# Softmax sums from ScalarE's natural exponentials, folded into the shift, with attention scheduled query chunk by query chunk

## The reference

```python
xn = layernorm(x)
Q, K, V = xn @ Wq.T, xn @ Wk.T, xn @ Wv.T            # 16 heads of 32
S = einsum('bhqd,bhkd->bhqk', rope(Q), rope(K)) * 32 ** -0.5
S = where(causal, S, -inf)
heads = einsum('bhqk,bhkd->bqhd', softmax(S), V)
x = x + heads @ Wo.T + (silu(xn @ Wg.T) * (xn @ Wu.T)) @ Wd.T
```

## Time and profile before

| | us |
|---|---|
| median of 3 runs | 2245.01 (2243.44 to 2249.74) |
| the profiled execution, its own time | 2243.66 |
| its span | 2241.8 |
| PE, busy | 2034.9 (91%) |
| DVE, busy | 1176.1 (52%) |
| ACT, busy | 737.9 (33%) |
| POOL, busy | 760.3 (34%) |
| granted TensorE clock, mean | 0.978 |

### The profile page before, as it was taken

The page is one execution under the profiler, slowest core; times in us unless marked ns, Lnnn a source line. Parts: engine busy times, 40 slices in busy tenths (PEclk is TensorE's granted clock), DMA queues, the critical chain, the costliest instruction groups (busy, mean ns, idle before and its releaser), DMA issues.

```text
span 2241.8 us, 34912 instructions
## 1 busy us (share of the span) xinstructions
PE 2034.9 (91%) x10176; PEld 1352.9 (60%) x10176; DVE 1176.1 (52%) x2458; ACT 737.9 (33%) x1357; POOL 760.3 (34%) x552
## 2 busy tenths in 40 slices
PE   4999999999899999999869999999997999999996
PEld 3756657566475646476557576674755746464764
DVE  5635637355555646374357265472736537282733
ACT  2242332423323342423322423324242242415242
POOL 3324324242321515153323143431423215142523
PEclk9999999999899999999979999999998999999998
DMA  3313103041130303041123041220411303030403
GB/s 136 79 32 95 43 28 94 15 114 43 38 74 28 89 19 98 10 118 30 53 103 96 11 104 33 54 83 9 113 34 43 85 11 98 10 98 17 126 24 122
DMA packets 72428, 140.67 MB, mean 63 GB/s; under 512 B 9328, under 2 KB 26736, under 8 KB 71152
## 3 DMA queue, kind: packets, MB, share of 16 engines
q1 hardware_dynamic: 72304, 139.25, 22.2%
HBM read 75.77 MB, written 4.19 MB: 36 GB/s over the span
## 4 chain that ended last, share of the span: by engine, by line
PE 44%; issue 26%; POOL 15%; DVE 6%; ACT 2%; SPq 2%; DMA 2%; DVEq 1%; POOLq 1%; ACTq 1%
PE D L900 10%; PE G L900 8%; PE S L969 7%; PE O L986 6%; PE U L900 6%; PE E L993 3%; POOL pr L745 3%; POOL swapped L727 3%; POOL pr L733 2%; ACT pr L639 2%; POOL wgl L698 2%; POOL hl L721 2%; SPq L576 2%; POOL wul L698 1%; PE S L953 1%
## 5 line engine op out<-in xcount | busy, mean ns | idle before, releaser
L639 ACT ACTIVATE pr<-S 128x512 f32<-128x512 f32 (+3 forms) x768 | 341.1, 489 | 293.7 <-PE S L969 292.0
L868 DVE TENSOR_TENSOR xres<-D,xres 128x512 f32<-128x512 f32 x352 | 242.2, 688 | 347.4 <-PE D L900 341.3
L721 POOL TENSOR_TENSOR hl<-tt,hh 128x512 fp32r<-128x512 f32 x108 | 138.9, 1286 | 550.2 <-ACT hh L663 550.0
L969 PE MATMUL S<-QS,KS 98*128 98x512 f32 (+2 forms) x768 | 240.5, 388 | 11.4 <-DMA QS<-mt 5.7
L969 PEld LDWEIGHTS S<-QS,KS 98*128 98x128 f32 x768 | 132.8, 188 | 192.1 <-ACT pr L639 171.0
L663 ACT CAST hh<-tt 128x512 fp32r<-128x512 f32 x108 | 67.0, 620 | 481.8 <-DVE tt L882 481.8
L745 POOL TENSOR_SCALAR_AFFINE_SELECT pr<-pr 128x512 f32<-128x512 f32 x128 | 81.2, 635 | 379.7 <-ACT pr L639 379.7
L986 PE MATMUL O<-pr,vh 128*32 128x512 f32 (+3 forms) x1536 | 163.8, 498 | 46.4 <-POOL pr L745 45.5
L858 DVE RECIPROCAL denom<-denom 128x256 f32<-128x256 f32 x64 | 109.1, 1730 | 181.0 <-ACT denom L646 181.0
L900 PE MATMUL G<-xh,wgh 128*128 128x512 f32 x432 | 177.6, 411 | 14.2 <-DVE tt L879 10.6
L900 PE MATMUL D<-wdh,hh 128*128 128x512 f32 x432 | 180.1, 417 | 4.1 <-DVE xres L868 3.2
(11 more groups left out here) (137 smaller groups left out, 3737.6 us busy)
## 6 DMA issues: line engine op xcount, KB each, us to landing
KS<-pr SPq DMA_DIRECT2D x192, 128.0 KB, 2.3
QS<-pr SPq DMA_DIRECT2D x192, 128.0 KB, 2.3
raw<-in_wgate_dram SPq DMA_DIRECT2D x29, 512.0 KB, 3.5
raw<-in_wup_dram SPq DMA_DIRECT2D x28, 512.0 KB, 3.7
raw<-in_wdown_dram SPq DMA_DIRECT2D x28, 512.0 KB, 3.4
raw<-in_wqk_dram SPq DMA_DIRECT2D x18, 512.0 KB, 3.4
vh<-val SPq DMA_DIRECT2D x16, 512.0 KB, 3.8
val<-in_x_dram SPq DMA_DIRECT2D x6, 1024.0 KB, 10.3
```

Source lines behind the costliest of these rows:

```text
L639: act.activation(pr[:, (i * HG + h) % 8, skip:W], S[h % 2][:, skip:W], ACT.Exp, scale=SCALE) \
L721: pool.tensor_tensor(hl[:, fc, :], tt[:, (blk * nfc + fc) % 2, :], hh[:, fc, :].bitcast(F32), ALU.subtract) \
L868: dve.tensor_tensor(xres[:, rt, :], d[:, :], xres[:, rt, :], ALU.add).then_inc(sem["v_dfree"], 1)
L969: pe.matmul(S[h % 2][:, first:W], KS[0:SHIFT, h, kb * P:(kb + 1) * P], QS[0:SHIFT, h, c * W + first:(c + 1) * W], start=True, stop=True).t ...
```

## The change

Five things change together.

1. *Sums.* After VectorE's row extreme (now a minimum, since the factor -32^-0.5 is multiplied into Q in `proj` and `rotate`), ScalarE takes the exponential of each natural score block in place in PSUM, with the minimum as bias and the row sum as accumulator output. For the second chunk the two parts' sums are joined by a few small operations (`parts`, `joined`). Then `log`: ScalarE takes the logarithm and VectorE subtracts the minimum and splits the result into halves; `flip` transposes it with PE. There is one `log` and one `flip` for each chunk. The transposed scores are then shifted by maximum plus logarithm, so their exponentials are the softmax itself.
2. *Gone:* `sums` on PE, the copy of the denominators, the reciprocals, the multiplication of the heads. `heads` is now one cast on ScalarE (`ah`) and one subtraction on VectorE (`al`); GpSimd's part in it is gone.
3. *Buffers.* `pr` holds four sets (`RING`); the transposed scores take turns in three banks (S0, S1, E). `swapped` and `xn` lie in `pr`.
4. *Order.* Natural scores go chunk by chunk (16 products for queries 0 to 511, then 32), and values two sets at a time, behind the four scores of the next set. MLP pieces are spread by `paced` over natural and transposed scores in proportion to needs that `NEED_NAT` and `NEED_ST` state. The last two sets' values stand behind the first projection (`V` in `ENDS`).
5. *Weights.* The raw buffers are fixed by kind: A, O and U share buffer 0, G and D buffer 1. The split of A moves ahead of the natural scores, that of O to natural product 24.

The core of the diff:

```diff
+RING = 4
-    return [[("nat", h, u)] for h in range(HG) for u in range(len(NAT))]
+    items = [([("nat", t)], NEED_NAT[w_ // P - 1]) for t, (_, _, _, _, w_) in enumerate(NAT)]
+    n0 = sum(x[0] == 0 for x in NAT)
+    items[n0 + 3][0].append(("log", 0))
+    items[n0 + 7][0].append(("flip", 0))
...
+NEED_NAT = (3, 4, 4, 4)
+NEED_ST = (2, 2, 3, 3)
+EDGE = {"turn0": (8, 4), "turn1": (6, 4), "tail0": (10, 14), "tail1": (7, 10)}
+ENDS = ("pVpwwxpxxpwwxpD", "pVpwwxpxxpwwxpD")
-SLOTS = {"open0": "", "turn0": "A0 G1 U0 O1 D0 G1 U0 D1", "tail0": "A0 G1 U0 O1 D0 G1 U0 D1",
-         "open1": "", "turn1": "O1 A0 G0 U1 D0", "tail1": "O1 A0 G1 U0 D1 G0 U1 D0 G1 U0 D1"}
+SLOT = {"A": 0, "O": 0, "U": 0, "G": 1, "D": 1}
...
 @block.scalar
+            def nat(n, t):
+                c, h, qb, part, w_ = NAT[t]
+                act.wait_ge(sem["v_max"], n("v_max", 1))
+                s, at = NB[t % 4][:, 0:w_], h * TPC + qb % TPC
+                act.activation(s, s, ACT.Exp, bias=mp[:, c + part, at:at + 1], scale=-1.0,
+                               accum_out=se[:, c + part, at:at + 1]).then_inc(sem["a_nat"], 1)
+            def log_(n, c):
+                if c:
+                    act.wait_ge(sem["v_join"], n("v_join"))
+                else:
+                    act.wait_ge(sem["a_nat"], n("a_nat"))
+                act.activation(lse[:, :], se[:, 0, :], ACT.Ln).then_inc(sem["a_log"], 1)
...
-                act.wait_ge(sem["p_pv"], n("p_pv"))
+                act.wait_ge(sem["p_pv"], n.at("p_pv", i - RING + 1))
-                act.copy(heads[:, :], O[:, :])
-                act.copy(denom[:, :], E[:, :]).then_inc(sem["a_heads"], 1)
+                act.wait_ge(sem["p_wo"], n("p_wo"))
+                act.copy(ah[:, :], O[:, :]).then_inc(sem["a_ah"], 1)
...
 @block.vector
+            def log_(n, c):
+                dve.wait_ge(sem["a_log"], n("a_log", 1))
+                dve.wait_ge(sem["p_flip"], n("p_flip"))
+                dve.tensor_tensor(lse[:, :], lse[:, :], low_[:, :] if c else mp[:, 0, :], ALU.subtract).then_inc(sem["v_lse"], 1)
...
+                dve.tensor_copy(mm[:, 0, :].bitcast(F32R), lse[:, :]).then_inc(sem["v_lse"], 1)
...
+                dve.tensor_tensor(mm[:, 1, :], lse[:, :], mm[:, 0, :], ALU.subtract).then_inc(sem["v_lse"], 1)
-                dve.reciprocal(denom[:, half], denom[:, half]).then_inc(sem["v_recip"], 1)
-                dve.tensor_tensor(heads[:, :], heads[:, :], denom[:, :], ALU.mult).then_inc(sem["v_heads"], 1)
+            def heads_(n, c):
+                dve.wait_ge(sem["a_ah"], n("a_ah", 1))
+                dve.tensor_tensor(al[:, :], O[:, :], ah[:, :].bitcast(F32), ALU.subtract).then_inc(sem["v_al"], 1)
...
 @block.tensor
-                    pe.wait_ge(sem["v_max"], n("v_max", -3))
+                    pe.wait_ge(sem["a_nat"], n("a_nat", -3))
+            def flip(n, c):
+                pe.wait_ge(sem["v_lse"], n("v_lse"))
+                pe.wait_ge(sem["v_dfree"], n("v_dfree", -1))
+                pe.transpose(Dk[n.dk()][:, 0:P], mm[:, :, :].rearrange("p a b -> p (a b)"), ident[:, :]) \
+                    .then_inc(sem["p_flip"], 1)
-                if i or h >= 2:
-                    pe.wait_ge(sem["a_exp"], n("a_exp", -1))
+                if k < 3:
+                    pe.wait_ge(sem["a_nat"], n("a_nat", (-3, -2, 0)[k]))
+                else:
+                    pe.wait_ge(sem["a_exp"], n.at("a_exp", k - 2))
-            def sums(n, i):
...
-                for h in range(HG):
-                    ins = pe.matmul(E[h * DH:(h + 1) * DH, skip:W], ones[:, :], pr[:, (i * HG + h) % 8, skip:W],
-                                    start=kb == 0, stop=kb == TPC * (c + 1) - 1)
```

More of the change, by code:

```diff
@@ L89, in weighted, with paced @@
 def weighted():
-    st = [[[("st", 0, h) for h in two] for two in ((0, 1), (2, 3))]]
-    st[0][1].append(("causal", 0))
-    for i in range(1, len(SETS) + 1):
-        scores = [("st", i, h) for h in range(HG)] if i < len(SETS) else []
-        if i < len(SETS) and diagonal(i):
-            scores.append(("causal", i))
-        now = [scores[:2] + [("pv", i - 1)], scores[2:] + [("sums", i - 1)]]
-        c, kb = SETS[i - 1]
-        if kb == TPC * (c + 1) - 1:
-            now[-1].append(("heads", c))
-        st.append(now)
-    return st
+    out = []
+    for i, (c, kb) in enumerate(SETS):
+        need = NEED_ST[min(TPC * (c + 1) - kb, TPC) - 1]
+        for two in ((0, 1), (2, 3)):
+            out.append(([("st", i, h) for h in two], need))
+        if diagonal(i):
+            out[-1][0].append(("causal", i))
+        if i == 0:
+            out[-2][0].append(("parts",))
+            out[-1][0].append(("joined",))
+        if i == 1:
+            out[-2][0].append(("log", 1))
+        if i == 2:
+            out[-2][0].append(("flip", 1))
+        if i and i % 2 == 0:
+            out.append(([("pv", i - 2), ("pv", i - 1)] + [("heads", SETS[i - 1][0])] * (SETS[i - 1][0] != c), 0))
+        if i == 6:
+            out += [(x, 0) for x in output(0)]
+    return out
+def paced(items, pieces):
+    total, owed, out = sum(need for _, need in items), 0, []
+    k = 0
+    for steps, need in items:
+        out.append(steps)
+        owed += need * len(pieces)
+        while k < len(pieces) and (k + 1) * total <= owed:
+            out.append(pieces[k])
+            k += 1
+    return out + pieces[k:]
 def projections():
@@ L486, in walk @@
                     n.bases = {}
+                    n.first = dict(n.n)
                     if times == 1:
@@ L855, in recip @@
[L855 to L862 removed]
+                dve.wait_ge(sem["v_lse"], n("v_lse"))
```

266 lines of the change are left out of this document (125 added, 141 removed).

## The result

The changed kernel takes 2329.1 us (median of 4 runs, 2322.8 to 2331.3) where the kernel before takes 2244.2 on the same chip: a ratio of 1.037, interval 1.034 to 1.040. It is 85 us slower. The prediction was 2124 us, faster, and its range ended at 2205. In the profiled execution the span went from 2241.8 to 2327.0 us and the granted clock from 0.978 to 0.931.

What follows compares the result with a forecast made beforehand. The prediction took the kernel as bound by PE's work. Gains of 6 x 5 (layer 0), 6 x 8.5 (layer 1) and 4 x 10 (tails) made 121 us off 2243.7, and 1.3 to the median: 2124 us, range 2055 to 2205.

Steps and rivals of the forecast that it cites:

- Removed from PE: All turns: matmuls on ones (10.3 us) and switches (2.0 us) leave PE, 12.3 us a turn, 197 us in all.
- The clock: Whole kernel: vanishing causal waits are replaced by one of like size at product 30, so no clock change is counted.
- Layer 1, natural stage: Layer-1 natural scores: ScalarE sets the pace at 33 us against 26 of PE work; 7 us lost, net +3.
- Layer 1, transposed stage: Layer-1 transposed scores: about 2 us waiting at the flip, 0.3 us lost a value pair, 1.8 in all.
- Layer 0, natural stage: Layer-0 natural scores: PE stands 2.7 us at product 26 and 4.8 at product 30 behind U's load; 8 with flip.
- Exponentials, tables: ScalarE: 48 natural exponentials a turn at 0.55 us, 26.3 us; four table loads a turn, 5.1 us.
- Tails: Four tails: 12.3 us and about 3 of waits go, 5 come back; a gain of 10 each.
- Rival C: Natural stage: in-place exponential with its read is not pipelined, 0.8 us each; slower, about 2260 us; chance 0.10.
- A: Whole kernel: half of the new waits are hidden, 2055 us, spread 2030 to 2090; chance 0.2.
- B: ScalarE table switches: each holds twice its 1.283 us row, 57 us more, 2181 us, spread 2155 to 2215; chance 0.2.

Runs made afterwards that it cites:

- the version with both edits: Changed kernel with values one set at a time and, in layer 0's equal turns, O split at natural product 10: 2266.3 us, ratio 1.012.
- the spread version: Changed kernel with single-set values, O at product 10 in every layer-0 turn, first chunk's output tiles spread over sets 6 to 9: 2263.4 us.
- the version without the log: The kernel with spread output tiles, its logarithm replaced by an exponential of scale 0 so no table is loaded for it: 2239.7 us, ratio 0.998.

## Why the prediction was wrong

By the turns, the sum had -5 for a layer-0 turn, -8.5 for a layer-1 turn and -10 for a tail; measured +2.1, +11.3 and +1.2. That makes 43, 119 and 45 us, the whole 206 between the predicted and the measured span.

- **The step that failed is the first one, "Removed from PE": 12.3 us a turn, 197 in all, "and nothing else ran beside them on PE", counted in full on the path.** The matmuls did leave, and of the cover that goes with them the step said that "nothing is lost if that cover goes, since it is work taken away". But in the layer-1 transposed stage ScalarE has 24.5 us of exponentials and GpSimd 9 of selects in a chain with PE, and the sums were PE's work while that chain ran. Alone, without any new work, their removal gave 13 us where this step had 149, and made each layer-1 turn 2.6 us longer. The list of waits was misread in "So the kernel is bound by the work that PE is given": PE's 4.8 us of waiting for exponentials did not mean that ScalarE was far ahead, only that the sums stood in between; without them they are 40.5.
- **The clock, "so I count nothing", was the second failure.** 222 us more at the lower level are up to 111 us; by the two pairs of like stages (0.28 and 0.42 us each) 62 to 93. The argument that like waits replace like was made for one stage of layer 0. New waits came in every stage of layer 1. This part and the first cannot be added as if apart, since the clock fell with the waits.
- **Layer 1, natural stage, 33 us.** 37.5 in the first turn, 43.0 in the next ones. PE's work of 26 us and 7 us lost were near: in turn 5 PE is idle 7.4 us, and of 35.6 busy at most 8.6 are stretch (0.20 x 43.0), so at least 27 are work. What was missing is that stretch. The choice "ScalarE sets the pace" was wrong all the same: with exponentials 11 us shorter in sum the stage lost 3.4. It goes at the pace of the chain product, minimum, exponential, next product, with tanh and its gate product in the same queue; which link holds longest, I have not settled. The step from 37.5 to 43.0 is the head of the stage, with 5 us of waits and 14 us at 0.51; the sum had 2 us for the stack there and nothing for the tanh.
- **Layer 1, transposed stage: 0.3 us lost a value pair, 1.8 in all.** Too small. Undoing the pairs gave 32 us over the kernel: 3.3 in a layer-1 turn, most of it in the transposed stage, about 3 in a tail, nothing in a layer-0 turn. The row of output tiles right behind a pair was not in the step. Spread out, it changed nothing more.
- **Layer 0, natural stage, 56 us with a stall behind U's load.** Measured 59.0. This step was right in place, cause and nearly in size: ScalarE's wait 5.5 us where 3.8 stood, PE's 0.8 at product 26 where 2.7 stood and its 3.1 at product 30 where 4.8 stood, and 1.4 for G's low half that it did not have. Moving O mended it, and the stage came to 52.5 in the version with both edits. Turn 1 took 140.1 us and not 131.1: 3 of these 9 lie here, 6 in the transposed stage and the end of the turn, 81.1 us for 75.1.
- **Exponentials, tables.** 0.55 us each and four loads a turn were right, though 341 over 768 is 0.444, a busy time without the overlaps; the 0.489 that the 0.55 goes by is the mean of the rows. Where the loads stand was not right, and leaving the log out gave 48 us, more than half of it in the tails, where my sum had 5 us each for everything new together.
- **Tails.** Predicted -10 each: 173.0, 206.3, 172.8 and 149.8 against 171.1, 205.4, 171.3 and 149.2. The sums' 12.3 were counted there too, and taking them out of the kernel before gave 2.2 a tail; single values gave 3 a tail, leaving the log out 6.
- **Rival C** had the sign only, 15 us slower where 85 were measured, and by a mechanism that did not occur: exponential and read start every 0.66 us and not every 0.8. That its sign came true is luck. A, the half of the waits hidden, is refuted. B's idle beside each load is not there. All that the loads cost in the changed kernel, 48 us, is less than the 57 that B put on top of their rows.

## What to carry to other kernels

An instruction on the bound engine need not be on the path: it is not, as far as its neighbours on that engine would otherwise wait for another: before counting it at full length, take it out in thought and ask whether the engine beside it, here ScalarE with 24.5 us of 44.2 and two banks, can deliver sooner. One run that leaves the work out of the old kernel shows it. Where a change replaces continuous PE work by many waits of one to three microseconds, expect PE's clock to fall with them, and count some 0.3 to 0.4 us for each microsecond at the lower level. Two sets of values in one row cost 32 us here; the output tiles behind them, spread out, gave nothing more.

## What I had not expected of the hardware

- The clock fell after short waits, with PE at work most of the time. In turn 9 PE waited 0.8 us, did one product and waited another 1.4 us, and from there the same gate matmuls start 0.43 us apart with rows of 0.63. The granted clock is 0.50 from 1404 to 1410 and 1.00 from 1418 to 1426, where they start 0.23 us apart. Order of time on PE:

```profile
1402.63 0.50 PE L990 MATMUL O<-KS,QS 96*128 96x512 f32 x1 [0.79 <-ACT O L646]
1404.52 0.79 PE L939 MATMUL G<-xh,wgh 128*128 128x512 f32 x1 [1.39 <-POOL wgl L718]
1405.11 0.63 PE L939 MATMUL G<-xl,wgh 128*128 128x512 f32 x1
1405.53 0.63 PE L939 MATMUL G<-xh,wgl 128*128 128x512 f32 x1
...
1425.22 0.39 PE L939 MATMUL G<-xl,wgh 128*128 128x512 f32 x1
1425.45 0.40 PE L939 MATMUL G<-xh,wgl 128*128 128x512 f32 x1
```

  The Trainium skill describes a clock that swings between its two levels when PE idles for short times between groups of matmuls that cycle through PSUM banks ("TensorE: Matmul & The Clock Gate", A second HAM failure mode: psum-queue depth-cycling). The trace agrees in kind, with waits of 0.79 and 1.39 us between such groups.
- A microsecond at the lower level cost less than half a microsecond: 0.42 us in the tail stage where PE was at work for 94% of the time, 0.28 in the transposed stage of layer 1. Executions of one and the same kernel say the same: the spread version took 2255.1 us at 0.949 and 2273.1 at 0.937, 56 us more at the lower level for 18 us, 0.32 each; the version without the log 2228.4 at 0.948 and 2248.4 at 0.937, 0.39 each.
- After a logarithm the next exponential needed a table load of its own, although the Trainium skill lists a set that holds both ("ScalarE: Activation LUTs", Table sets). Of the 32 logarithms of this trace at least 30 are followed by a load for an exponential, so the table loaded for them did not serve the exponential, or the second load was needless; the trace does not say which.
